# A routed two-expert layer on one core: turning the expert tiles through DRAM and VectorE instead of on TensorE

## The chip, the cores and the metric

One core of a Trainium2 chip. The metric is the device time of one execution in microseconds (us), the median of three runs. The engines are TensorE (PE, with its weight loads as PEld), VectorE (DVE), ScalarE (ACT), GpSimd (POOL) and SyncE (SP), which here only issues DMAs. A line number such as L1182 is a line of the kernel before.

## What is computed

The input is x, 8 x 512 tokens of 256 features. xn is its layer norm. The output is

```
x + attention(xn) + experts(xn)
attention: 16 heads of 16; A = tril(1 + q.k/4 + (q.k)^2/32), y = A v / rowsum(A), then y Wo^T
experts:   top 2 of 8 by xn Wg, weights by softmax over the two
           out[n] += w * ( silu(xn W1[e]) * (xn W2[e]) ) W3[e]      W1, W2: 256x512, W3: 512x256
```

Everything is float32.

## The kernel before

All engines run programs of their own, written out by hand (`sync_program`, `gpsimd_program`, `scalar_program`, `vector_program`, `tensor_program`), tied by semaphores: `p_*` are raised by PE, `v_*` by DVE, `a_*` by ACT, `g_*` by POOL, `d_*` by DMAs (16 for each that has landed). Within a program the order of the text is the order of the work; nothing overtakes.

The first 300 us do the attention in 32 quarters (`NQ`) and route the tokens. POOL scatters each token's normalised row (256 features, 8 gates, its number: `XW` = 272 words) twice into `xs_scr` in DRAM, once for each of its experts, so that the rows of one expert can be gathered. The second half works through `NT` = 71 tiles of 128 rows. A tile has one expert (`texp`, read into a register). The experts need at most 71 tiles; a tile beyond what they need is filled with spare rows and scattered to spare rows of `out`. The weights of the experts are loaded at the border of the two halves (`load_w12`, 16 units of 512 KB; `load_w3`, 8 of 512 KB), and each is split into a high and a low float32r part, since every product is made of three passes, high x high, high x low, low x high.

One tile t takes these steps:

- `gather(t)` (POOL, L485): an indirect DMA brings 128 rows into `xg`, a ring of `GR` = 4. `transpose_g(t)` (PE, L1171) turns them with two transposes into bank 4. `expert_x(t)` copies them as `xgh` (ACT, L619) and `xgl` (DVE, L979), and DVE copies the gates into `xw` (L984).
- `up(t, 0)` and `up(t, 1)` (PE, L1182): six matmuls each, for the silu branch and for the gate branch, into banks 0 to 3.
- `hs` is made by ACT's silu (L638) and DVE's product (L1009). `transpose_s(t)` (PE, L1191) turns it with four transposes into bank 5. `high_s` (ACT, L625) and `low_s` (DVE, L988) copy it as `sTh` and `sTl`. All of `xgh`, `xgl`, `hs`, `sTh`, `sTl` are single buffers.
- `down(t)` (PE, L1203): twelve matmuls into bank 6 or 7. `weigh_y(t)` (DVE, L996) multiplies by the row's gate into `yo` (two buffers). `scatter(t)` (POOL, L496) adds the rows to `out` in DRAM with an accumulating indirect DMA; it waits on `d_sc` for the scatter before, as two experts may hold the same token.

PE's order in the loop over t, the part that sets everything else, is:

```
up(t, 0); transpose_s(t - 1); up(t, 1); transpose_g(t + 1); down(t - 1)
```

DVE's is `low_s(t - 1)`, product of t, `expert_x(t + 1)`, for the first eight tiles also `w3_low(t + 1)` (L711) and `w12_low` (L706, up to t = 5), then `weigh_y(t - 1)`; ACT's follows it. POOL keeps four gathers ahead. SP has no work after its last load: at the border it issues `load_w3` (6 and 7 after `v_te`), `load_w12(14)`, waits for the last attention rows to reach `out` (`out_sent(LAST)`), issues `load_w12(15)` (L336), and then only waits for the scatters.

## Time and profile before

| | |
|---|---|
| median of 3 runs | 668.18 us (668.07 to 668.24) |
| the profiled execution, first to last instruction | 665.4 us |
| PE busy | 641.8 us, 96% |
| PE weight loads | 496.5 us, 75% |
| DVE busy | 410.6 us, 62% |
| ACT busy | 341.6 us, 51% |
| POOL busy | 344.1 us, 52% |
| DMA | 64.07 MB, mean 96 GB/s |

The profile gives the span of one execution, from its first to its last instruction; the time of a run is 2.8 us longer than that span. Busy shares are means over both halves of the kernel; the rows further down are of single stretches. A matmul's duration includes time in which the next one already streams, so the pace of PE is read from starts and from the chain of waits. The chain follows the work that ended last back from the end, each step to what released it.

### The profile page before, as it was taken

What the parts mean: (1) busy time and instruction counts of PE and PEld (TensorE: products, weight loads), DVE (VectorE), ACT (ScalarE), POOL (GpSimd) and SP (SyncE); (2) the same over time, 40 slices, a digit from 0 to 9 for tenths busy, and PEclk for the clock granted to TensorE, in tenths of its full rate; (3) what the DMA queues carried; (4) which work ended last, traced back from release to release, by engine and by line L of the source; (5) the groups of instructions that cost most, each with busy time, mean ns of one, the idle gap of its engine ahead of it and who ended that gap; (6) DMA issues with size and microseconds to landing.
All of it is one profiled execution on the core that took longest, in us unless ns stands there. A gap on an engine that the chain in (4) does not pass through costs nothing.

```text
span 665.4 us, 16423 instructions
## 1 busy us (share of the span) xinstructions
PE 641.8 (96%) x5414; PEld 496.5 (75%) x5414; DVE 410.6 (62%) x1067; ACT 341.6 (51%) x515; POOL 344.1 (52%) x381
## 2 busy tenths in 40 slices
PE   8899999999999999999999999999999999999994
PEld 7555666666666666657888888888888888888883
DVE  6777788787878585777975444444544445444452
ACT  3668878787877686766642232322323223232331
POOL 3265655546463736473465555455545555455542
PEclk9999999999999999999999999999999999999998
DMA  4653555554443435447633434333333433333332
GB/s 134 141 133 99 127 153 130 152 130 147 93 136 77 128 85 154 118 150 249 207 59 58 66 51 66 50 57 60 58 59 50 66 51 57 58 51 58 58 50 25
DMA packets 37775, 64.07 MB, mean 96 GB/s; under 512 B 8289, under 2 KB 25825, under 8 KB 37697
## 3 DMA queue, kind: packets, MB, share of 16 engines
q0 software_dynamic: 16704, 28.12, 22.0%
q1 hardware_dynamic: 20432, 34.24, 20.2%
q8 instruction: 50, 0.82, 0.5%
q10 hardware_dynamic: 560, 0.66, 0.3%
q14 instruction: 29, 0.23, 0.1%
HBM read 27.72 MB, written 22.68 MB: 76 GB/s over the span
## 4 chain that ended last, share of the span: by engine, by line
PE 87%; DVE 4%; DMA 2%; ACT 2%; issue 2%; SPq 1%; ACTq 0%; POOL 0%; POOLq 0%; DVEq 0%
PE banks L1182 29%; PE banks L1203 15%; PE banks L1056 10%; PE banks L1038 8%; PE banks L1076 7%; PE banks L1191 5%; PE banks L1085 4%; PE banks L1120 3%; PE banks L1171 2%; PE banks L1105 1%; PE banks L1111 1%; DMA K<-Kt 1%; ACT T L533 1%; DVE xTl L740 1%; PE banks L1094 1%
## 5 line engine op out<-in xcount | busy, mean ns | idle before, releaser
L496 POOL DMA_INDIRECT out<-yo,xw x71 | 112.2, 1581 | 154.4 <-DVE yo L996 76.6
L625 ACT ACTIVATE sTh<-banks 128x512 fp32r<-128x512 f32 x71 | 42.5, 598 | 192.4 <-PE banks L1191 186.6
L476 POOL TENSOR_SCALAR_AFFINE_SELECT T<-T 128x512 f32<-128x512 f32 x128 | 80.8, 642 | 108.5 <-ACT T L539 43.1
L988 DVE TENSOR_TENSOR sTl<-banks,sTh 128x512 fp32r<-128x512 f32 x71 | 49.0, 691 | 118.9 <-ACT sTh L625 118.9
L1182 PE MATMUL banks<-w12h,xgh 128*128 x284 | 118.0, 415 | 0.6 <-DVE xgl L979 0.6
L1182 PE MATMUL banks<-w12l,xgh 128*128 x284 | 112.2, 395 | 0.0
L1182 PE MATMUL banks<-w12h,xgl 128*128 x284 | 112.1, 395 | 0.0
L485 POOL DMA_INDIRECT xg<-xs_scr,glist x71 | 72.4, 1020 | 21.5 <-issue 20.0
L1056 PE MATMUL banks<-T,vau 128*17 128x512 f32 (+3 forms) x1024 | 75.6, 434 | 0.9 <-POOL T L476 0.9
L467 POOL DMA_INDIRECT xs_scr<-xb,slots x64 | 64.3, 1004 | 18.7 <-issue 10.0
L1038 PE MATMUL banks<-Q,K 32*128 32x256 f32 (+2 forms) x1024 | 70.5, 358 | 3.5 <-DMA K<-Kt 2.2
L525 ACT ACTIVATE T<-banks 128x1024 f32<-128x1024 f32 x64 | 62.1, 1026 | 12.5 <-PE banks L1038 11.9
L533 ACT ACTIVATE T<-banks 128x768 f32<-128x768 f32 x64 | 48.5, 810 | 27.2 <-PE banks L1038 27.2
L1182 PEld LDWEIGHTS banks<-w12h,xgl 128*128 128x128 f32 x284 | 53.3, 188 | 12.0
L1056 PEld LDWEIGHTS banks<-T,vau 128*17 128x17 f32 x1024 | 26.0, 97 | 46.3 <-issue 38.4
L1182 PEld LDWEIGHTS banks<-w12h,xgh 128*128 128x128 f32 x284 | 53.8, 189 | 7.8 <-issue 1.0
L1038 PEld LDWEIGHTS banks<-Q,K 32*128 32x128 f32 x1024 | 38.6, 183 | 27.1 <-ACT T L525 12.7
L1182 PEld LDWEIGHTS banks<-w12l,xgh 128*128 128x128 f32 x284 | 53.9, 190 | 6.3
L996 DVE TENSOR_SCALAR yo<-banks,xw 128x256 f32<-128x256 f32 x71 | 34.3, 483 | 39.0 <-PE banks L1203 31.2
L539 ACT ACTIVATE T<-banks 128x768 f32<-128x768 f32 x64 | 48.7, 810 | 18.0 <-PE banks L1038 16.1
L1009 DVE TENSOR_TENSOR hs<-banks,hs 128x512 f32<-128x512 f32 x71 | 49.1, 692 | 10.2 <-PE banks L1182 0.9
L1203 PE MATMUL banks<-w3h,sTh 128*128 x284 | 51.1, 302 | 0.8 <-ACT sTh L625 0.8
(174 smaller groups left out, 1222.3 us busy)
## 6 DMA issues: line engine op xcount, KB each, us to landing
Q<-Q SPq DMA_DIRECT2D x128, 64.0 KB, 2.4
w12r<-w SPq DMA_DIRECT2D x16, 512.0 KB, 4.2
out<-xa SPq DMA_DIRECT2D x16, 256.0 KB
w3r<-w SPq DMA_DIRECT2D x8, 512.0 KB, 8.7
K<-Kt SPq DMA_DIRECT2D x124, 32.0 KB
xa<-x SPq DMA_DIRECT2D x7, 512.0 KB, 4.7
xg<-xs_scr,glist POOLq DMA_INDIRECT x71
out<-yo,xw POOLq DMA_INDIRECT x71
```

What stands on the lines that cost most here:

```text
L467: e.indirect_dma_start(xs_d, bass.IndirectOffsetOnAxis(slots[:, k, 4 * b + blk:4 * b + blk + 1].bitcast(U32), 0), xb[b % 2][:, blk, :], No ...
L476: e.affine_select(out=v, in_=v, pattern=[[0, 4], [1, P]], compare_op=ALU.is_ge, fill=-1.0, base=0, channel_multiplier=-1).then_inc(s["g_mk ...
L485: e.indirect_dma_start(xg[:, t % GR, :], None, xs_d, bass.IndirectOffsetOnAxis(glist[:, t:t + 1].bitcast(U32), 0)).then_inc(s[f"d_g{t % GR ...
L496: e.indirect_dma_start(out, bass.IndirectOffsetOnAxis(xw[:, t % 4, NE:NE + 1].bitcast(U32), 0), yo[:, t % 2, :], None, compute_op=ALU.add) ...
L525: e.activation(T0[n % 2][:, 2 * h:2 * h + 2, :], banks[:, 2 * h:2 * h + 2, :], ACT.Square, scale=0.25, bias=1.0).then_inc(s["a_s"], 1)
L533: e.activation(T1[:, 2 * h:2 * h + 2, :], banks[:, 2 * h:2 * h + 2, 0:384], ACT.Square, scale=0.25, bias=1.0).then_inc(s["a_s"], 1)
L988: e.tensor_tensor(sTl[:], banks[:, 5, :], sTh[:].bitcast(F32), ALU.subtract).then_inc(s["v_st"], 1)
L1009: e.tensor_tensor(hs[:], banks[:, 2 * (t % 2) + 1, :], hs[:], ALU.mult).then_inc(s["v_mu"], 1)
L1038: i = e.matmul(banks[:, r, c0:c0 + w], K2[rr, g, h, jm * P:(jm + 1) * P], Q2[g][rr, h, p, 512 - w:512], start=(p == 0), stop=(p == 1))
L1056: i = e.matmul(banks[32 * r:32 * r + HA, 4, 512 - w:512], vau[b % 2][:, jm, 4 * qd + r, :], v[:, r, :], start=(jm == 0), stop=(jm == 2), s ...
L1182: i = e.matmul(banks[:, 2 * (t % 2) + m, :], a[:, k, :], w[:, bass.ds(expert[t] * 4 + (2 * k + m), 1), :], start=(k == 0 and n == 0), stop ...
L1203: i = e.matmul(banks[:, 6 + t % 2, 0:256], a[:, k * P:(k + 1) * P], w[:, bass.ds(expert[t] * 4 + k, 1), :], start=(k == 0 and n == 0), sto ...
```

## The change

Feature q of a row is now paired with its neighbour: the host lays the rows of `w12` and `w3` out as (P, 2) and (P, 4) where they were (2, P) and (4, P), so that partition p holds features 2p, 2p+1 (or 4p to 4p+3). A turn by 128 is then split in two. A store writes the tile's rows to DRAM (`x_turn`, `h_turn`) by column groups, a load reads them back so that 32 column positions and 4 row groups share the partitions, and DVE turns blocks of 32x32 from that buffer (`xq`, `hq`) into PSUM. ACT and DVE copy out of PSUM as before, with other access patterns.

- For tiles 4 (`TX`) and on, `store_x`, `load_x` (SP) and `turn_x` (DVE) take the place of `transpose_g`; for tiles 8 (`TS`) to 68 (below `TE`), `store_h`, `load_h` and `turn_s` that of `transpose_s`. Tiles 69 and 70 turn the product on PE again.
- From tile 8 on, `down` runs three tiles (`LAG`) behind `up`, `low_s` and `high_s` two tiles behind, and `expert_x` two tiles ahead.
- `xgh`, `xgl`, `hs`, `sTh`, `sTl` have two buffers and `xw` eight (`XR`); `xq` and `hq` have one.
- Gathers are issued in another order, up to nine tiles ahead of the scatter.
- `scatter(t)` waits for scatter t - 2, and for scatter t - 1 only where `held` says so: where t is the first tile of an expert, or a tile beyond those needed. `holds` computes that table on DVE in the first tile's iteration; POOL reads a word of it for each tile, and issues a small `mark` operation.
- `load_w3(6)` and `load_w3(7)` wait for `v_hold` in place of `v_te`. The descriptor scratch of POOL's DMAs is set to 4096 bytes.

The diff, cut to its core (`x_bank`, `s_bank` are the PSUM views; left out are the register and semaphore declarations and the constants of `holds`):

```diff
+TX = 4
+TS = 8
+TE = NT - 2
+LAG = 3
+XR = 8
...
+        sTh = rm.take("sTh", 1024, F32R, (2, 512))
+        sTl = rm.take("sTl", 1024, F32R, (2, 512))
...
+        hs = rx.take("hs", 1024, F32, (2, HID))
...
+        hq = rx.take("hq", 512)
+        xgh = rx.take("xgh", 512, F32R, (2, 256))
+        xgl = rx.take("xgl", 512, F32R, (2, 256))
+        xq = rx.take("xq", 256)
+        xw = rx.take("xw", XR * 16, F32, (XR, 16))
...
+        def x_bank(t):
+            v = banks[:, 4, 0:256]
+            return v if t < TX else v.rearrange("p (t j c) -> p j c t", t=4, j=2)
+
+        def x_turned(tile, t):
+            v = tile[:, t % 2, :]
+            return v if t < TX else v.rearrange("p (j c t) -> p j c t", j=2, t=4)
+
+        def s_bank(t):
+            v = banks[:, 5 if t < TE else 4 if t == TE else 2, :]
+            return v.rearrange("p (t k c) -> p k c t", t=4, k=4) if TS <= t < TE else v
+
+        def s_turned(tile, t):
+            v = tile[:, t % 2, :]
+            return v.rearrange("p (k c t) -> p k c t", k=4, t=4) if TS <= t < TE else v
...
-            e.wait_ge(s["v_te"], 1)
+            e.wait_ge(s["v_hold"], 1)
...
+            def store_x(t):
+                e.wait_ge(s[f"d_g{t % GR}"], 16 * (t // GR + 1))
+                e.dma_start(x_d[t % 4].rearrange("r p f -> p r f"),
+                            xg[:, t % GR, 0:D].rearrange("p (r f) -> p r f", r=4)).then_inc(s[f"d_sx{t % 2}"], 16)
+
+            def load_x(t):
+                e.wait_ge(s[f"d_sx{t % 2}"], 16 * ((t - TX) // 2 + 1))
+                if t > TX:
+                    e.wait_ge(s["v_tx"], t - TX)
+                e.dma_start(xq[:], x_d[t % 4].rearrange("r (c t) f -> (r c) (t f)", t=4)).then_inc(s["d_lx"], 16)
+
+            def store_h(t):
+                e.wait_ge(s["v_mu"], t + 1)
+                e.dma_start(h_d[t % 4].rearrange("r p f -> p r f"),
+                            hs[:, t % 2, :].rearrange("p (r f) -> p r f", r=4)).then_inc(s[f"d_sh{t % 2}"], 16)
+
+            def load_h(t):
+                e.wait_ge(s[f"d_sh{t % 2}"], 16 * ((t - TS) // 2 + 1))
+                if t > TS:
+                    e.wait_ge(s["v_th"], t - TS)
+                e.dma_start(hq[:], h_d[t % 4].rearrange("r (c t) f -> (r c) (t f)", t=4)).then_inc(s["d_lh"], 16)
+
+            store_x(TX)
+            for t in range(NT):
+                if TS <= t < TE:
+                    store_h(t)
+                if TS <= t - 1 < TE:
+                    load_h(t - 1)
+                if TX <= t + 3 < NT:
+                    load_x(t + 3)
+                if TX < t + 5 < NT:
+                    store_x(t + 5)
+            for u in range(2):
+                e.wait_ge(s[f"d_sc{u}"], 16 * ((NT + 1 - u) // 2))
 
...
-                    e.wait_ge(s["p_gt"], t - GR + 1)
+                    if t - GR < TX:
+                        e.wait_ge(s["p_gt"], t - GR + 1)
+                    else:
+                        e.wait_ge(s[f"d_sx{t % 2}"], 16 * ((t - GR - TX) // 2 + 1))
...
-                else:
-                    e.wait_ge(s["d_sc"], 16 * t)
-                e.indirect_dma_start(out, bass.IndirectOffsetOnAxis(xw[:, t % 4, NE:NE + 1].bitcast(U32), 0), yo[:, t % 2, :], None,
-                                     compute_op=ALU.add).then_inc(s["d_sc"], 16)
+                if t >= 3:
+                    if t == 3:
+                        e.wait_ge(s["v_hold"], 1)
+                    else:
+                        e.wait_ge(s["g_hold"], t - 3)
+                    count = 16 * ((t - 1) // 2)
+                    landed = e.value_load(held[0:1, t - 1:t], min_val=count, max_val=count + 16)
+                    e.wait_ge(s[f"d_sc{(t - 1) % 2}"], landed)
+                    e.tensor_tensor(mark[:], minus[:], minus[:], ALU.add).then_inc(s["g_hold"], 1)
+                    e.wait_ge(s[f"d_sc{t % 2}"], 16 * (t // 2))
+                elif t:
+                    e.wait_ge(s[f"d_sc{(t - 1) % 2}"], 16)
+                e.indirect_dma_start(out, bass.IndirectOffsetOnAxis(xw[:, t % XR, NE:NE + 1].bitcast(U32), 0), yo[:, t % 2, :], None,
+                                     compute_op=ALU.add).then_inc(s[f"d_sc{t % 2}"], 16)
...
-            for t in range(GR):
-                gather(t)
+            ahead = 0
             for t in range(NT):
-                if t + GR < NT:
-                    gather(t + GR)
+                upto = t + 5 if t == 0 else t + 6 if t < TS else t + 9
+                while ahead <= min(upto, NT - 1):
+                    gather(ahead)
+                    ahead += 1
                 scatter(t)
...
-            for t in range(NT + 1):
-                if t >= 1:
+            for t in range(NT):
+                if 1 <= t <= TS:
                     high_s(t - 1)
-                if t < NT:
-                    e.wait_ge(s["p_h"], t + 1)
-                    e.activation(hs[:], banks[:, 2 * (t % 2), :], ACT.Silu).then_inc(s["a_si"], 1)
+                e.wait_ge(s["p_h"], t + 1)
+                if 2 <= t < TS + 2:
+                    e.wait_ge(s["p_st"], t - 1)
+                elif TS + 2 <= t < TE + 2:
+                    e.wait_ge(s[f"d_sh{t % 2}"], 16 * ((t - 2 - TS) // 2 + 1))
+                e.activation(hs[:, t % 2, :], banks[:, 2 * (t % 2), :], ACT.Silu).then_inc(s["a_si"], 1)
                 if t == 0:
                     w3_high(0)
-                if t + 1 < NT:
+                if t + 1 < TX:
                     expert_x(t + 1)
+                if t - 2 >= TS:
+                    high_s(t - 2)
+                if TX <= t + 2 < NT:
+                    expert_x(t + 2)
                 if t + 1 < NE:
                     if t == 0:
                         e.wait_ge(s["p_av"], NQ)
@@ -651,10 +753,12 @@
                     elif u == 14:
                         e.wait_ge(s["p_o"], 2 * NBATCH)
                     w12_high(u)
+            high_s(NT - 2)
+            high_s(NT - 1)
...
+            def holds():
+
+                e.wait_ge(s["c_hold"], 2)
+                then(e.tensor_scalar(change[:], iota[:, 0:72], end[:, NE - 1:NE], None, ALU.is_ge))
+                then(e.tensor_tensor(part[:, 0:71], tf[:, 1:72], tf[:, 0:71], ALU.subtract))
+                then(e.tensor_tensor(change[:, 1:72], change[:, 1:72], part[:, 0:71], ALU.max))
+                then(e.scalar_tensor_tensor(held[:, 0:71], change[:, 1:72], 16.0, before[:, 0:71], ALU.mult, ALU.add), "v_hold")
...
+            def turn_x(t):
+                e.wait_ge(s["d_lx"], 16 * (t - TX + 1))
+                e.wait_ge(s["v_gt"], t)
+                e.transpose(banks[:, 4, 0:256], xq.rearrange("p (t m j) -> p t j m", t=4, j=2)).then_inc(s["v_tx"], 1)
+
+            def turn_s(t):
+                e.wait_ge(s["d_lh"], 16 * (t - TS + 1))
+                e.wait_ge(s["v_st"], t)
+                e.transpose(banks[:, 5, :], hq.rearrange("p (t m k) -> p t k m", t=4, k=4)).then_inc(s["v_th"], 1)
...
+            def gate_x(t):
                 e.wait_ge(s[f"d_g{t % GR}"], 16 * (t // GR + 1))
-                if t >= 4:
-                    e.wait_ge(s["d_sc"], 16 * (t - 3))
-                e.tensor_copy(xw[:, t % 4, :], xg[:, t % GR, D:XW]).then_inc(s["v_xw"], 1)
+                if t >= XR:
+                    e.wait_ge(s[f"d_sc{t % 2}"], 16 * ((t - XR) // 2 + 1))
+                e.tensor_copy(xw[:, t % XR, :], xg[:, t % GR, D:XW]).then_inc(s["v_xw"], 1)
...
             expert_x(0)
+            gate_x(0)
+            gated = 1
             step("y", LAST, 1)
             w12_low(UNITS)
             step("o", LAST, 0)
-            for t in range(NT + 1):
-                if t >= 1:
+            for t in range(NT):
+                if 1 <= t <= TS:
                     low_s(t - 1)
-                if t < NT:
-                    e.wait_ge(s["a_si"], t + 1)
-                    e.wait_ge(s["p_g"], t + 1)
-                    e.tensor_tensor(hs[:], banks[:, 2 * (t % 2) + 1, :], hs[:], ALU.mult).then_inc(s["v_mu"], 1)
-                if t + 1 < NT:
+                e.wait_ge(s["a_si"], t + 1)
+                e.wait_ge(s["p_g"], t + 1)
+                e.tensor_tensor(hs[:, t % 2, :], banks[:, 2 * (t % 2) + 1, :], hs[:, t % 2, :], ALU.mult).then_inc(s["v_mu"], 1)
+                if t + 1 < TX:
                     expert_x(t + 1)
+                if TS <= t - 2 < TE:
+                    turn_s(t - 2)
+                if TX <= t + 2 < NT:
+                    turn_x(t + 2)
+                while gated <= min(t + 1 if t < 2 else t + 3, NT - 1):
+                    gate_x(gated)
+                    gated += 1
+                if t - LAG >= TS:
+                    weigh_y(t - LAG)
+                if t - 2 >= TS:
+                    low_s(t - 2)
+                if TX <= t + 2 < NT:
+                    expert_x(t + 2)
                 if t == 0:
                     step("o", LAST, 1)
                     w3_low(0)
+                    holds()
                 if t + 1 < NE:
                     w3_low(t + 1)
                 if UNITS + 1 + t < 16:
                     w12_low(UNITS + 1 + t)
-                if t >= 1:
+                if 1 <= t <= TS:
                     weigh_y(t - 1)
+            low_s(NT - 2)
+            weigh_y(NT - 3)
+            low_s(NT - 1)
+            weigh_y(NT - 2)
+            weigh_y(NT - 1)
...
-            for t in range(1, NT + 1):
-                if t < NT:
-                    expert_of(t)
-                    up(t, 0)
+            for t in range(1, NT):
+                expert_of(t)
+                up(t, 0)
                 if t == 1:
                     for m in range(3):
                         e.wait_ge(s[f"m{m}"], USED[m])
-                transpose_s(t - 1)
-                if t < NT:
-                    up(t, 1)
-                if t + 1 < NT:
+                if t <= TS or t == TE + 1:
+                    transpose_s(t - 1)
+                up(t, 1)
+                if t + 1 < TX:
                     transpose_g(t + 1)
-                if t <= NE:
-                    e.wait_ge(s["v_tl"], t)
-                down(t - 1)
+                if t <= TS:
+                    if t <= NE:
+                        e.wait_ge(s["v_tl"], t)
+                    down(t - 1)
+                elif t - LAG >= TS:
+                    down(t - LAG)
+            transpose_s(NT - 1)
+            for t in range(NT - LAG, NT):
+                down(t)
...
-        "w12": w12.reshape(NE, 2, P, 2, HID).transpose(2, 0, 1, 3, 4).reshape(P, NE * 4, HID),
-        "w3": np.asarray(L0_ffn_W3).reshape(NE, 4, P, D).transpose(2, 0, 1, 3).reshape(P, NE * 4, D),
+        "w12": w12.reshape(NE, P, 2, 2, HID).transpose(1, 0, 2, 3, 4).reshape(P, NE * 4, HID),
...
-    nc = bacc.Bacc("TRN2", target_bir_lowering=False, num_devices=1)
+    nc = bacc.Bacc("TRN2", target_bir_lowering=False, num_devices=1, dynamic_dma_scratch_size=4096)
```

## Rows read from the trace of the kernel before

**Rows 1.** Stretches: length, busy PE, PEld, DVE, ACT, POOL, clock, DMA share, GB/s

```profile
341.00:652.00 311.00, 311.00 (x1911) 271.02 (x1910) 146.41 (x320) 94.29 (x192) 164.21 (x127) 1.00 0.35 56
```

**Rows 2.** Chain of waits, one tile: start us, us, what

```profile
644.27 1.39 PE banks L1182 x6
645.66 0.44 PE banks L1191 x4
646.10 1.40 PE banks L1182 x6
647.49 0.22 PE banks L1171 x2
647.71 1.43 PE banks L1203 x12
```

**Rows 3.** Timeline of DVE and of PE, first expert tiles: start us, us, engine

```profile
296.76 0.22 DVE L772 CAST glist<-banks 128x72 int32<-128x72 f32 x1
...
321.09 0.41 DVE L979 TENSOR_TENSOR xgl<-banks,xgh 128x256 fp32r<-128x256 f32 x1
...
323.13 1.22 DVE L706 TENSOR_TENSOR w12l<-w12r,w12h 128x1024 fp32r<-128x1024 f32 x1
324.27 0.48 DVE L996 TENSOR_SCALAR yo<-banks,xw 128x256 f32<-128x256 f32 x1
...
326.25 0.64 PE L1203 MATMUL banks<-w3h,sTl 128*128 x4
```

**Rows 4.** Timeline of PE and of POOL, the end

```profile
652.20 0.63 PE L1203 MATMUL banks<-w3h,sTh 128*128 x4
...
654.69 1.55 POOL L496 DMA_INDIRECT out<-yo,xw  x1 [3.09 <-DVE yo L996]
659.25 1.55 POOL L496 DMA_INDIRECT out<-yo,xw  x1 [3.00 <-DMA out<-yo,xw]
```

**Rows 5.** Groups by line on DVE, 340 to 650 us: busy, mean ns, idle before

```profile
L1009 DVE TENSOR_TENSOR hs<-banks,hs 128x512 f32<-128x512 f32 x64 | 44.3, 692 | 9.1 <-PE banks L1182 0.2
...
L996 DVE TENSOR_SCALAR yo<-banks,xw 128x256 f32<-128x256 f32 x64 | 30.9, 484 | 36.9 <-PE banks L1203 29.9 <-DMA out<-yo,xw 7.0
L979 DVE TENSOR_TENSOR xgl<-banks,xgh 128x256 fp32r<-128x256 f32 x64 | 26.5, 414 | 0.0
L984 DVE COPY xw<-xg 128x16 f32<-128x16 f32 x64 | 11.2, 175 | 0.0
```

**Rows 6.** Groups by line on POOL, 341 to 650 us

```profile
L496 POOL DMA_INDIRECT out<-yo,xw x64 | 101.2, 1581 | 125.4 <-DVE yo L996 70.2 <-DMA out<-yo,xw 42.4 <-PE banks L1171 7.1
L485 POOL DMA_INDIRECT xg<-xs_scr,glist x62 | 61.5, 992 | 18.9 <-issue 17.4 <-DVE xw L984 1.5
```

**Rows 7.** DMA queues, 289 to 294 us and 304 to 320 us: packets, MB, share

```profile
q1 hardware_dynamic: 272, 0.26, 16.4%
...
q1 hardware_dynamic: 1759, 4.99, 86.3%
```

**Rows 8.** DMA queues, 359 to 648 us

```profile
q0 software_dynamic: 11399, 15.98, 35.0%
```

**Rows 9.** DMA issues: KB each, us from issue to landing

```profile
wo_r<-wo SPq DMA_DIRECT2D x1, 256.0 KB, 2.6
...
out<-zero SPq DMA_DIRECT2D x1, 128.0 KB, 5.1
```

**Rows 10.** Instructions of line 336 on SP: ns, first and last start

```profile
L336 SPq DMA_DIRECT2D w12r<-w x16: 328/484/1644, 39.0 to 320.2; - x16
```

**Rows 11.** DMA, 318 to 328 us in 40 slices of 0.25 us

```profile
GB/s 447 414 426 406 418 434 401 446 393 442 410 410 442 410 361 311 328 442 360 393 279 156 148 119 205 139 33 156 204 217 17 0 0 0 0 0 0 0 0 0
```

**Rows 12.** Stretches at the end, columns as in rows 1

```profile
658.00:660.00 2.00, 0.00 (x0) 0.00 (x0) 0.00 (x0) 0.00 (x0) 0.76 (x1) 1.00 0.01 1
...
662.00:665.40 3.40, 0.00 (x0) 0.00 (x0) 0.00 (x0) 0.00 (x0) 0.00 (x0) 0.50 0.18 28
```

**Rows 13.** DMA queues, 656 to 665 us

```profile
q0 software_dynamic: 288, 0.26, 26.9%
```

More of the change, by code:

```diff
@@ L157, in build @@
         banks = ctx.enter_context(nc.psum_tensor("banks", [P, 8, 512], F32))
-        rm = Region(344, A0)
+        rm = Region(344, Q1)
         xg = rm.take("xg", GR * XW, F32, (GR, XW))
-        xgh = rm.take("xgh", 256, F32R, (2, P))
-        xgl = rm.take("xgl", 256, F32R, (2, P))
-        hs = rm.take("hs", 512)
-        sTh = rm.take("sTh", 512, F32R)
-        sTl = rm.take("sTl", 512, F32R)
-        yo = rm.take("yo", 512, F32, (2, D))
-        xw = rm.take("xw", 64, F32, (4, 16))
-        rq = Region(344, A0)
+        sTh = rm.take("sTh", 1024, F32R, (2, 512))
+        sTl = rm.take("sTl", 1024, F32R, (2, 512))
+        yo = rm.take("yo", 512, F32, (2, D))
+        rx = Region(Q1, A0)
+        hs = rx.take("hs", 1024, F32, (2, HID))
+        at_hq = rx.at
+        hq = rx.take("hq", 512)
[3 more added lines that the diff above has]
+        xw = rx.take("xw", XR * 16, F32, (XR, 16))
+        held = rx.take("held", 72, I32)
+        mark = rx.take("mark", 4)
+        rh = Region(at_hq, at_hq + 512)
+        before_i = rh.take("before_i", 72, I32)
+        before = rh.take("before", 72)
+        change = rh.take("change", 72)
+        rq = Region(344, Q1)
         K2 = rq.take("K2", 2048, F32R, (2, 2, 512))
@@ L446, in gpsimd_program @@
             e.memset(zero[:], 0.0).then_inc(s["c_z"], 1)
+            e.wait_ge(s["c_hold"], 1)
+            e.tensor_copy(before[:], before_i[:]).then_inc(s["c_hold"], 1)
             e.wait_ge(s["c_z"], 1)
@@ L1181, in up @@
                     for n, (a, w) in enumerate(((xgh, W12h), (xgh, W12l), (xgl, W12h))):
[L1182 removed]
+                        i = e.matmul(banks[:, 2 * (t % 2) + m, :], a[:, t % 2, k * P:(k + 1) * P], w[:, bass.ds(expert[t] * 4 + (2 * k + m), 1), :],
                                      start=(k == 0 and n == 0), stop=(k == 1 and n == 2))
@@ L1202, in down @@
                     for k in range(4):
-                        i = e.matmul(banks[:, 6 + t % 2, 0:256], a[:, k * P:(k + 1) * P], w[:, bass.ds(expert[t] * 4 + k, 1), :],
+                        i = e.matmul(banks[:, 6 + t % 2, 0:256], a[:, t % 2, k * P:(k + 1) * P], w[:, bass.ds(expert[t] * 4 + k, 1), :],
                                      start=(k == 0 and n == 0), stop=(k == 3 and n == 2))
```

53 lines of the change are left out of this document (33 added, 20 removed).

## The prediction

> **What bounds the kernel now.** The sums are against the profiled execution (span 665.4 us); the median of the runs is 668.2 us, 2.8 us more, and I carry that 2.8 unchanged. From the page I took the busy shares, then a table of stretches, then the chain of waits. From 341 to 652 us TensorE (PE) is busy for the whole of the stretch at full granted clock, VectorE (DVE) for 47%, GpSimd (POOL) for 53% [rows 1]. So in the expert part PE sets the pace and everything else fits beside it. The chain shows one tile, five pieces: six up matmuls 1.40, four turns of the gated product 0.44, six up matmuls 1.39, two turns of the gathered rows 0.22, twelve down matmuls 1.43, together 4.88 us [rows 2]. Two ends differ. At the beginning DVE runs almost without a gap, because it splits weights too [rows 3]; at the end the last scatter waits for the one before it to land [rows 4].
>
> **What it removes.** Turns of rows leave PE for tiles 4 to 70, 67 x 0.22 = 14.7 us; turns of the gated product for tiles 8 to 68, 61 x 0.44 = 26.8 us [rows 2]. Together **-41.5 us**, and PE's tile becomes 1.40 + 1.39 + 1.43 = 4.22 us. It is all gain only if each new helper keeps a period of 4.22 us.
>
> **DVE per tile.** Today two 128x512 operations (hs and sTl) of 0.692 and 0.414 + 0.484 + 0.175, in all 2.46 us [rows 5]. It adds a 32x32 turn of 128x512 and one of 128x256. The trace has none; the nearest rows are the DVE operations of the same size that touch PSUM, 0.69 and 0.41 us. Lower end half of these (no second operand to read), upper end twice, should a turn run at half rate. Taken: those rows, 1.1, sum 3.6 us (3.0 to 4.7). ACT gets no new instruction, only another source to wait for.
>
> **POOL per tile.** Gather 0.99 and scatter 1.58 with 0.3 ahead of each [rows 6] are 3.2 us; the new register read and the 128x4 `mark` operation are as small as DVE's 0.175 us copy [rows 5]; from nothing to 0.3 each: 3.2 to 3.8 us, taken 3.5. It fits under 4.22. A scatter that landed alone took 4.56 us until the next one started [rows 4]; that serial chain would no longer fit, and the second scatter in flight removes it except where an expert changes (seven times, one tile's delay, covered by the spare POOL time) and at the end (below).
>
> **The DMA trips.** Per tile 128 KB go out in 512 packets of 256 bytes and come back in 128 of 1 KB; 256 KB go out in 512 packets of 512 bytes and come back in 128 of 2 KB. A stretch with stores in 1 KB packets gives 16.4% x 5 us x 16 / 272 = 48 ns a packet; one with mostly 4 KB packets gives 86.3% x 16 us x 16 / 1759 = 125 ns for 2.84 KB in the mean [rows 7]. A line through both gives 15, 26, 48 and 92 ns for the four sizes, so 7.7 + 13.3 + 6.1 + 11.8 = 38.9 us over 16 engines, 2.4 us per tile. That is also about the low end (bytes at the 1 KB rate: 2.3). The high end is that no packet costs less than a 1 KB one: 4.2 us. I take 2.4, since the two rows differ almost in proportion to bytes. Gathers and scatters already take 35.0% x 289 us / 59.3 tiles = 1.7 us [rows 8]. Sum 4.1 of 4.22 us: it just fits, and it is the thinnest margin here. The Trainium skill speaks against the change: its page "DMA: Bandwidth & Descriptors" (Specifications) asks for at least 512 bytes per transfer for line rate and says that below this the engine reads, modifies and writes. No packet of data under 1 KB is in this trace, so it can't be checked; the sum by that rule is worked as the first rival, without it.
>
> **The loop through one buffer.** `hq` is single, so load_h(t-1) waits until turn_s(t-2) is done, and turn_s(t-1) waits for the load. A lone 256 KB load took 2.6 us from issue to landing, and 128 KB among other transfers 5.1 [rows 9]. Ahead of it in SP's queue is store_h(t), issued 0.6 us earlier with 0.8 us of data; with that and a share of the scatter I take 3.3. Then 0.7 + 0.1 + 3.3 = 4.1 us, again just under 4.22. SP itself issues four DMAs of some 0.5 us [rows 10], 2 us. As both margins are thin, I put **+5 us** (0.08 x 61) for periods that slip; nothing to 40 are the ends (40: the period stays 4.88).
>
> **The beginning.** `holds` puts four small dependent operations (0.22 us each, as the 0.22 us cast) [rows 3] on DVE at about 313 us, ahead of low_s(0), for which PE already waits: **+0.9**. SP reaches store_x(4) only behind load_w12(15), which it issues at 320.2 because it first waits for the last output rows [rows 10]. The engines are full until about 323.3 us [rows 11], so store_x(4) lands near 325, load_x(4) (2.6 and some) near 327.7, and turn_x(4) ends near 328.1. DVE wants it in its iteration 2, right after xgl at 321.5 plus 0.9 [rows 3]. Queued behind it on DVE are the gate copies, xgl(4), two weight splits (which wait for ACT, itself stuck at expert_x(4)), weigh_y(1) and low_s(2): 0.4 + 0.5 + 1.7 + 1.2 + 0.4 + 0.6, low_s(2) ends at 332.9. PE wants it at the third part of down(2), near 326.9. **+6.0 us** PE idle; bounds 2 (the landings 2 us quicker, the splits overlapped) and 9. After it DVE's iterations of 5.1 us against PE's 4.66 cost **+1.3** until the splits end. PE at rest loses its clock: at the end of the trace PE does nothing from 658 us on, the granted clock is still 1.00 up to 660, and from 662 it is 0.50, the 1.2 GHz level [rows 12]. I put **+1.0** (0 to 3). The skill's page "TensorE: Matmul & The Clock Gate" (What's actually happening) states the same drop to half at rest; the trace agrees.
>
> **The end.** The down projections are three tiles behind, but at tiles 9 and 10 PE does no down, so its total work is the same and the last up matmuls end 2 x 1.43 = 2.9 us earlier than the savings alone give. From the end of the last up matmul, p = 652.2, the execution before needs 13.15 us. Now weigh_y(67) follows down(67) at p + 2.0 and scatter(67) starts at p + 2.4. By counting the reference's inputs, the experts fill 9, 9, 8, 8, 8, 8, 8 and 9 tiles, 67 in all; tiles 67 to 70 are padding, and `held` makes each of their scatters wait for the one before. Three steps of 4.56 + 0.15 and the 6.1 us that the last scatter needs to the end [rows 4] give p + 22.6. That is +9.4 - 2.9 = **+6.5 us**.
>
> **Sum**: -41.5 + 0.9 + 6.0 + 1.3 + 1.0 + 6.5 + 5 = -20.8, from 668.2 to **647 us**.
>
> **Rivals.** *DMA engines are the bound (slower than before).* If packets of 256 bytes cost as much as 1 KB ones, store_x takes 1.54 instead of 0.48, the tile 2.4 + 1.05 + 1.7 = 5.2 us, and the total is 668.2 - 41.5 + 15.7 + 61 x 0.98 = 702; if part of the 1.7 is waiting (two scatters by themselves were 26.9% x 9 us = 2.4, 1.2 each [rows 13]), about 4.9 and 684. It turns slower where the period passes 4.64 (25.8 us of net gain over 61 tiles is 0.42), that is at 2.9 us of new DMA time per tile. For it: the sum without it is already 98% of the period. Against: 400 GB/s with the engines full [rows 11], while the new sum is about 1.06 MB in 4.22 us, 250 GB/s. *The hq loop.* The load takes 3.6 to 4.2 under its own traffic: periods 4.4 to 5.0, total 653 to 690. For: 5.1 us in a contended stretch. Against: 2.6 alone. *The ends cost little*: the stall of DVE doesn't reach PE and the periods hold: 668.2 - 41.5 + 6.5 + 0.9 + 2 = 636. *DVE turns at half rate*: 4.7 us a tile, 61 x 0.48 in place of the 5, 671. That the turns stay on PE can't be: the code issues none there.
>
> **How the numbers follow.** Forecast (640 to 654) 0.42, ends cheap 0.10, hq loop 0.20 (0.13 faster, 0.02 same, 0.05 slower), DMA bound 0.20 (0.01 same), DVE slow 0.08 (0.02 faster, 0.02 same, 0.04 slower). Changes within 0.2%, 1.3 us, are about what a measurement of this kernel can't tell from none. Faster 0.42 + 0.10 + 0.13 + 0.02 = 0.67, same 0.05, slower 0.28. The range is 635 to 686: it leaves out only the worse part of the DMA case and a little below. The cases on the faster side alone lie between 635 and 660.
>
> **What would show it.** In the changed profile: the chain of a middle tile has 1.40, 1.39, 1.43 and no turn; DVE turns of about 0.69 and 0.41; PE idle of some 6 us once between 322 and 333; four scatters 4.7 us apart at the end; DMA share near 0.9 in the middle with some 230 GB/s or more; landing of load_h near 3.3. PE idle in each tile released by sTh or sTl, whose own releaser is the DMA of `hq`, shows the loop; DMA share at 0.98 or over with periods near 5 shows the first rival; DVE busy near 100% the last. The forecast is wrong if the middle period isn't 4.2 to 4.4.

## The result, and the profile after

The changed kernel takes 689.64 us in the median of four runs (687.1 to 691.13), the kernel before 668.21 beside it (668.07 to 669.03): 1.0314 times as long, 95% interval 1.0292 to 1.0337. The forecast of 647 us and its range to 686 were both wrong, and so was the direction. The profiled execution has a span of 686.9 us (688.6 as timed), against 665.4 before. Single runs of the kernels below that lie over 1.5% above a kernel's fastest are left out of the ratios; one does, 683.8 us for the turn without a step. The page of the changed kernel, its counts, chain and the group of the turn:

```profile
span 686.9 us, 16518 instructions
PE 630.1 (92%) x5036; PEld 468.2 (68%) x5036; DVE 485.1 (71%) x1199; ACT 335.4 (49%) x515; POOL 356.4 (52%) x451
DMA packets 123794, 113.63 MB, mean 165 GB/s; under 512 B 46688, under 2 KB 104032, under 8 KB 123712
...
PE 39%; DMA 30%; DVE 12%; issue 11%; ACT 3%; SPq 2%; DVEq 1%; POOL 1%; ACTq 0%; POOLq 0%
DMA hq<-h_turn 23%; PE banks L1199 10%; PE banks L1181 8%; PE banks L1219 7%; DVE banks L1097 6%; PE banks L1228 3%; PE banks L1263 3%; DMA out<-yo,xw 2%; PE banks L1326 2%; PE banks L1248 1%; DMA out<-xa 1%; PE banks L1254 1%; ACT T L620 1%; DVE hs L1133 1%; PE banks L1348 1%
...
L1097 DVE STREAM_TRANSPOSE banks<-hq 128x512 f32<-128x512 f32 x61 | 67.2, 1101 | 82.1 <-DMA hq<-h_turn 82.0
```

PE is 11.7 us less busy, yet the span is longer. Up matmuls (L1326) and down matmuls (L1348) have nearly left the chain, and a DMA, the load of `hq`, holds 23% of it.

The start of the product `hs(t)` on DVE is a good milestone for tile t, since both kernels do it once a tile. Read from the DVE timelines of the two kernels:

| stage | before | after | difference |
|---|---|---|---|
| up to hs(0) | 309.5 | 312.1 | +2.6 |
| hs(0) to hs(8) | 40.2 | 50.6 | +10.4 |
| hs(8) to hs(64) | 273.4 | 274.7 | +1.3 |
| hs(64) to hs(70) | 29.4 | 27.8 | -1.6 |
| hs(70) to the end | 12.9 | 21.7 | +8.8 |

Most of the first 2.6 us doesn't belong to the change: in this execution the granted clock was 0.66 between 20 and 30 us. Of the ten kernels below, which have the same first part or nearly, the four at full clock there reach hs(0) at 308.5 to 309.2 us, the four at 0.83 at 309.6 to 310.6, and the two at 0.66 at 310.6 and 311.1. Everything else is two fixed costs at the ends and a middle that gained nothing.

**The middle.** Stretches of the changed kernel (columns as in [rows 1]):

```profile
316.00:341.00 25.00, 18.48 (x91) 15.55 (x90) 17.45 (x31) 10.52 (x18) 6.20 (x5) 0.86 0.72 221
...
400.00:500.00 100.00, 93.77 (x493) 75.73 (x492) 71.35 (x146) 28.74 (x63) 55.66 (x61) 1.00 0.94 216
```

PE is busy 94% instead of 100% (a matmul's duration reaches into the next one, so its waits look shorter than they are); the DMA share went from 0.35 to 0.94. Between 400 and 660 us the chain of waits has almost no matmul in it. A piece of it (start us, us, what):

```profile
442.34 3.62 DMA hq<-h_turn
445.96 0.46 issue
446.42 1.11 DVE banks L1097
...
447.59 4.23 DMA hq<-h_turn
451.82 0.02 issue
451.84 1.12 DVE banks L1097
...
453.03 3.68 DMA hq<-h_turn
```

Load, turn, load, turn: the one buffer `hq` is a loop. Read from the timelines of SP and DVE over 430 to 600 us, SP issues the load of `hq` within 0.2 us of the end of the turn before it in 35 of 36 tiles, and DVE stands waiting for it in 35. From its issue to the start of its turn a load takes 3.71 us in the mean (2.6 to 4.5), the turn 1.10, and some 0.1 lies between: 4.9 us a tile. (The chain doesn't follow this loop all the way; in places it goes over the store of the product, with some 2.4 us of "issue" in front of the same load.) Between hs(24) and hs(64) the period is 4.93 us, where it was 4.88. The DVE groups of 400 to 600 us say how that looks on DVE (busy us, mean ns, idle before):

```profile
L1097 DVE STREAM_TRANSPOSE banks<-hq 128x512 f32<-128x512 f32 x41 | 45.2, 1102 | 54.9 <-DMA hq<-h_turn 54.9
...
L1092 DVE STREAM_TRANSPOSE banks<-xq 128x256 f32<-128x256 f32 x41 | 17.2, 420 | 0.3 <-DMA xq<-x_turn 0.3
```

DVE stands 1.3 to 1.4 us a tile in front of `turn_s`, waiting for the load, and the turn itself takes 1.10 us, not 0.69. The turn of half as many elements takes 0.42. The DMA queues of the same stretch (packets, MB, share of the 16 engines):

```profile
q1 hardware_dynamic: 54600, 32.02, 57.6%
q0 software_dynamic: 7755, 10.97, 35.7%
```

**The beginning.** DVE of the changed kernel (start us, us, what):

```profile
315.48 0.25 DVE L984 TENSOR_SCALAR change<-iota,end 128x72 f32<-128x72 f32 x1
...
316.31 0.23 DVE L987 SCALAR_TENSOR_TENSOR held<-change,before 128x71 int32<-128x71 f32 x1
...
324.90 0.41 DVE L1101 TENSOR_TENSOR xgl<-banks,xgh 128x256 fp32r<-128x256 f32 x1
330.52 0.46 DVE L1092 STREAM_TRANSPOSE banks<-xq 128x256 f32<-128x256 f32 x1 [5.21 <-DMA xq<-x_turn]
```

The four operations of `holds` are there; then DVE is idle for 5.21 us in front of `turn_x(4)`, with weight splits queued behind it. PE feels it at 329.4 us (start us, us, what):

```profile
328.07 0.40 PE L1326 MATMUL banks<-w12l,xgh 128*128 x1
328.31 0.40 PE L1326 MATMUL banks<-w12h,xgl 128*128 x1
...
334.08 1.22 PE L1348 MATMUL banks<-w3h,sTh 128*128 x4 [4.68 <-DVE w3l L815]
...
337.25 0.63 PE L1326 MATMUL banks<-w12l,xgh 128*128 x1
337.68 0.63 PE L1326 MATMUL banks<-w12h,xgl 128*128 x1
```

It waits 4.68 us for the low part of a weight that DVE splits behind `turn_x(4)`, and comes back slow: up matmuls start 0.43 us apart instead of 0.24. The granted clock is 0.50, the 1.2 GHz level, from 334 to 340 us, and 0.96 from 340 to 343.

**The end.** POOL of the changed kernel:

```profile
664.89 1.55 POOL L582 DMA_INDIRECT out<-yo,xw  x1 [0.46 <-POOL mark L578]
...
669.71 1.55 POOL L582 DMA_INDIRECT out<-yo,xw  x1 [0.70 <-POOL mark L578]
...
682.27 1.55 POOL L582 DMA_INDIRECT out<-yo,xw  x1 [0.15 <-issue]
```

These are scatters 66, 67 and 70; 68 and 69 start at 673.99 and 678.08. From scatter 67 on, each `mark` is released by the landing of the scatter before, so they come some 4.35 us apart. Five scatters stand behind the last up matmul, which ends at 664.9 us, where [rows 4] had two behind theirs.

### The profile page after: what moved, and what is told of

Same layout as the page of the kernel before. It is cut to its first block, busy times and chain, and to the rows that moved or that the text cites. A ratio compares the mean times of both kernels' runs of the same rounds, so it can differ in the third digit from the quotient of the medians.

```text
span 686.9 us, 16518 instructions
## 1 busy us (share of the span) xinstructions
PE 630.1 (92%) x5036; PEld 468.2 (68%) x5036; DVE 485.1 (71%) x1199; ACT 335.4 (49%) x515; POOL 356.4 (52%) x451
## 3 DMA queue, kind: packets, MB, share of 16 engines
q0 software_dynamic: 16704, 28.12, 21.6%
## 4 chain that ended last, share of the span: by engine, by line
PE 39%; DMA 30%; DVE 12%; issue 11%; ACT 3%; SPq 2%; DVEq 1%; POOL 1%; ACTq 0%; POOLq 0%
DMA hq<-h_turn 23%; PE banks L1199 10%; PE banks L1181 8%; PE banks L1219 7%; DVE banks L1097 6%; PE banks L1228 3%; PE banks L1263 3%; DMA out<-yo,xw 2%; PE banks L1326 2%; PE banks L1248 1%; DMA out<-xa 1%; PE banks L1254 1%; ACT T L620 1%; DVE hs L1133 1%; PE banks L1348 1%
## 5 line engine op out<-in xcount | busy, mean ns | idle before, releaser
L1326 PE MATMUL banks<-w12h,xgh 128*128 x284 | 118.8, 418 | 8.1 <-issue 4.3
L1097 DVE STREAM_TRANSPOSE banks<-hq 128x512 f32<-128x512 f32 x61 | 67.2, 1101 | 82.1 <-DMA hq<-h_turn 82.0
L1326 PE MATMUL banks<-w12h,xgl 128*128 x284 | 111.6, 393 | 0.0
L1326 PE MATMUL banks<-w12l,xgh 128*128 x284 | 111.5, 393 | 0.0
L1326 PEld LDWEIGHTS banks<-w12h,xgh 128*128 128x128 f32 x284 | 53.7, 189 | 28.1 <-issue 19.1
L1348 PE MATMUL banks<-w3h,sTh 128*128 x284 | 51.1, 302 | 20.1 <-ACT sTh L720 14.0
L578 POOL TENSOR_TENSOR mark<-minus 128x4 f32<-128x4 f32 x68 | 13.3, 196 | 105.6 <-DMA out<-yo,xw 87.2
L1348 PEld LDWEIGHTS banks<-w3h,sTh 128*128 128x128 f32 x284 | 41.9, 189 | 37.9 <-issue 35.6
L1326 PEld LDWEIGHTS banks<-w12h,xgl 128*128 128x128 f32 x284 | 53.6, 189 | 11.7
L1326 PEld LDWEIGHTS banks<-w12l,xgh 128*128 128x128 f32 x284 | 53.7, 189 | 8.7
L626 ACT ACTIVATE T<-banks 128x768 f32<-128x768 f32 x64 | 48.8, 810 | 18.5 <-PE banks L1181 16.5
```

Source lines behind the costliest of these rows:

```text
L626: e.activation(T2[:, 2 * h:2 * h + 2, :], banks[:, 2 * h:2 * h + 2, P:512], ACT.Square, scale=0.25, bias=1.0).then_inc(s["a_s"], 1)
L1097: e.transpose(banks[:, 5, :], hq.rearrange("p (t m k) -> p t k m", t=4, k=4)).then_inc(s["v_th"], 1)
L1326: i = e.matmul(banks[:, 2 * (t % 2) + m, :], a[:, t % 2, k * P:(k + 1) * P], w[:, bass.ds(expert[t] * 4 + (2 * k + m), 1), :], start=(k == ...
L1348: i = e.matmul(banks[:, 6 + t % 2, 0:256], a[:, t % 2, k * P:(k + 1) * P], w[:, bass.ds(expert[t] * 4 + k, 1), :], start=(k == 0 and n == ...
```

## Experiments

Theory L: the middle is the loop through `hq`, load plus turn. Rival D: the 16 DMA engines are full. Two more questions are what the small packets cost and whether the costs at the ends can be had back. Periods are read between hs(24) and hs(64) of each profile (or the two milestones named), as above. Expectations speak of the kernels by what they change; those of the first four were written before any of them had run.

**A second buffer for `hq`.** The load waits for the turn two tiles back.

```diff
-        hq = rx.take("hq", 512)
+        hq = rx.take("hq", 1024, F32, (2, 512))
...
-                if t > TS:
-                    e.wait_ge(s["v_th"], t - TS)
+                if t > TS + 1:
+                    e.wait_ge(s["v_th"], t - TS - 1)
```

Each buffer has its own load semaphore, and for room the descriptor scratch is 2048 bytes; that wasn't changed by itself.

> The changed kernel with hq in two buffers, so that load_h(t) waits for turn_s(t-2) instead of turn_s(t-1) (the descriptor scratch of POOL's DMAs is halved to 2048 bytes to make room). Loop theory: the period of 4.88 us is load_h (3.7) + turn_s (1.10) + 0.1 in series, and falls to what PE allows, 4.2 to 4.4; total about 689.6 - 59 x 0.55 = 657. Engine theory: the 16 DMA engines, busy 0.94 of the time, are the bound; the period can't fall below 0.94 x 4.88 = 4.6, and the total stays at 674 or more, with a DMA share of 0.98 or over.

Measured: 664.6 us (659.07 to 667.73, seven runs), 0.9938 of before (0.9903 to 0.9974), 25 us better than the change. Stretch and queues from 430 and 400 us on:

```profile
430.00:600.00 170.00, 163.78 (x906) 140.37 (x905) 133.35 (x264) 53.68 (x112) 105.19 (x115) 1.00 0.98 235
```

```profile
q1 hardware_dynamic: 59496, 34.83, 65.7%
q0 software_dynamic: 8542, 12.00, 31.9%
```

The period falls to 4.52 us with the same traffic per tile, so full engines were not what held the change at 4.93: theory L holds for it. The idle time before `turn_s` goes from 1.4 to 0.2 us a tile. But the 4.22 us of PE aren't reached, and the total lies between the two forecasts, 657 and 674. The engines are now busy for 0.98 of the time, 0.98 x 4.52 = 4.4 us of engine time a tile, so D is one candidate for what comes next. It is a soft bound: the same packets took 0.94 x 4.93 = 4.6 us in the change, so share times period isn't a fixed amount of work.

**A turn without a step in its reads.** `turn_s` reads 32 neighbouring words where it took every fourth. It turns other 32x32 blocks than the reference needs, so the gated product that goes into the down projection is a permuted one; the work is otherwise the same.

```diff
-                e.transpose(banks[:, 5, :], hq.rearrange("p (t m k) -> p t k m", t=4, k=4))
+                e.transpose(banks[:, 5, :], hq.rearrange("p (t k m) -> p t k m", t=4, k=4))
```

> The changed kernel, but turn_s reads hq without a step (k outside m instead of m outside k); the blocks it turns are then not those of the reference, all transfers and counts are the same. It is to tell whether the 1.10 us of turn_s, against 0.42 for half as many elements in turn_x, comes from the step of 4 words of its reads: then it falls to about 0.70. Loop theory: the period falls by those 0.4 us, total about 689.6 - 59 x 0.4 = 666. Engine theory: turn_s gets shorter but the waits for hq grow by the same, total 676 or more.

Measured: 679.48 us (671.88 to 683.8), ratio 1.0202 (1.0163 to 1.0241). The group of the turn, 430 to 600 us, beside the 1102 ns above:

```profile
L1097 DVE STREAM_TRANSPOSE banks<-hq 128x512 f32<-128x512 f32 x38 | 27.4, 722 | 17.0 <-DMA hq<-h_turn 16.8
```

The step in the reads costs 0.38 us per turn, and the period from hs(24) on is 4.57, which is 0.36 less than the change's, as a loop would have it. As a test of L this run is weak, though. From hs(8) to hs(24) the period is 4.85, as in the change (4.84); from 430 to 600 us DVE waits for `hq` in only half of the tiles, with the engines at 0.99. The profiled execution (671.88) was the fastest of the four, and the median is 10 us under the change where L said 24: it lies where the engine theory had put it, at 676 or more. The price of the step is shown; that its removal is worth as much in every execution is not.

**Rows turned on PE, product through DRAM.** It takes one of the two trips away, and with it the stall at tile 4.

```diff
-TX = 4
+TX = NT
...
-            store_x(TX)
...
-                upto = t + 5 if t == 0 else t + 6 if t < TS else t + 9
+                upto = t + 5 if t == 0 else t + 6 if t < TS else t + 8
```

> Half of the change alone: the gathered rows are turned on PE in all tiles (no store_x, load_x, turn_x), the gated product still goes through DRAM with the single hq. PE's tile is 4.44 us. The stall at tile 4 and its slow clock go, 8 us. Loop theory with the load slowed by the other transfers: without 0.85 us of DMA time per tile the load takes 2.9 to 3.2, the loop 4.1 to 4.4, PE is the bound, total 689.6 - 8 - 59 x 0.44 = 656. If the load's time is its own and not contention (3.7 stays), the period stays 4.88 and the total is about 681. DMA share falls to about 0.75.

Measured: 656.31 us (655.71 to 659.98), ratio 0.9852 (0.9819 to 0.9885). Its chain, and its stretch:

```profile
508.79 3.48 DMA hq<-h_turn
512.27 0.02 issue
512.29 1.11 DVE banks L1096
```

```profile
430.00:600.00 170.00, 169.17 (x971) 148.25 (x970) 120.93 (x224) 54.07 (x112) 104.21 (x113) 1.00 0.80 176
```

The engines are at 0.80, far from full, and still the chain from 430 to 600 us is load and turn. The load takes 3.35 us in the mean (2.5 to 4.3) instead of 3.71, and the period, 4.54, is shorter by the same 0.4. So the loop alone, without full engines, holds a period above PE's 4.44; and the load was shorter with less traffic around it. The total of 656 was forecast, but with PE as the bound and a load of 2.9 to 3.2; that part was wrong.

**The same, with a second buffer for `hq`.** `xgh` and `xgl` go back to one buffer each to make room.

```diff
-TX = 4
+TX = NT
...
-        hq = rx.take("hq", 512)
-        xgh = rx.take("xgh", 512, F32R, (2, 256))
-        xgl = rx.take("xgl", 512, F32R, (2, 256))
+        hq = rx.take("hq", 1024, F32, (2, 512))
+        xgh = rx.take("xgh", 256, F32R, (1, 256))
+        xgl = rx.take("xgl", 256, F32R, (1, 256))
```

> As the kernel with the gathered rows on PE, and hq in two buffers (xgh and xgl are single again, as before, to make room). Both theories say that nothing but PE bounds the middle: period 4.44, total 668.2 - 61 x 0.44 + 1.2 (holds) + 6.5 (end) = 649. It is equal to the kernel with a single hq if the loop there already fits under PE's period, and faster than it by what the loop still costs.

Measured: 651.55 us (650.54 to 652.9), ratio 0.9769 (0.9748 to 0.9789). Its chain:

```profile
508.73 2.75 PE banks L1326 x12
511.49 0.23 PE banks L1315 x2
511.71 1.44 PE banks L1348 x12
```

Here the chain is PE alone, 2.75 + 0.23 + 1.44 = 4.42, and the period 4.44: exactly the 0.44 us of the product's turns less than before. The descriptor scratch is 4096 bytes here, so the second buffer helps without that change too. From hs(69) to the end it needs 26.0 us, against 17.8 before.

**Eight tiles' rows turned on PE first.** One number of the change, `TX`, goes from 4 to 8, so that the first load of `xq` comes after the weights.

```diff
-TX = 4
+TX = 8
```

> The changed kernel with TX = 8: the rows of tiles 4 to 7 are turned on PE too, so nothing waits for the DMA queue behind the last weights. If the start costs what the prediction says, the time from DVE's product of tile 0 to that of tile 8 falls from 50.6 us to about 42 (40.2 before, and 1.1 for holds, 0.7 for the first turns on DVE), the clock stays full, and the total falls by 8.5 us to about 681; the middle keeps its period of 4.93. If the stall only hides a wait that comes anyway (weights that are late), it falls by less than 3.

Measured: 675.96 us (674.09 to 678.03), ratio 1.0123 (1.0091 to 1.0155). The stretch that held the stall:

```profile
316.00:341.00 25.00, 24.59 (x146) 21.64 (x147) 22.89 (x38) 14.72 (x23) 14.18 (x11) 1.00 0.63 166
```

PE is busy for 24.59 of 25 us instead of 18.48, and the clock is full. From hs(0) to hs(8) it takes 42.0 us instead of 50.6: 8.6 us back. The middle stays as it was (period 4.92, DMA share 0.94). Between the two profiled executions 13.2 us lie; 3.6 more of them are before the first tile, where the change's profile had its slow stretch, and 0.9 behind hs(70).

**The stores in long packets.** Beside the second `hq` buffer, rows are stored in packets of 1 KB and products in packets of 2 KB. The layout in DRAM is then another, so rows and products that are turned are not those of the reference; bytes, loads and turns are the same in number.

```diff
-                e.dma_start(x_d[t % 4].rearrange("r p f -> p r f"),
-                            xg[:, t % GR, 0:D].rearrange("p (r f) -> p r f", r=4))
+                e.dma_start(x_d[t % 4].rearrange("r (a b) f -> (r a) (b f)", b=4),
+                            xg[:, t % GR, 0:D])
```

> The changed kernel with two buffers for hq (and a descriptor scratch of 2048 bytes), and with both stores written to DRAM row by row, in packets of 1 KB and 2 KB in place of 256 and 512 bytes: the same bytes, a quarter of the packets. The blocks that DVE turns are then not those of the reference. It tells packets from bytes in the DMA engines' bound (share 0.98, period 4.52 with two buffers). If small packets cost extra (21 and 27 ns against 12 and 23 for their bytes), the engines' time per tile falls from 4.4 to about 4.0 and the period to PE's 4.2 to 4.25, total 664.6 - 59 x 0.3 = 647. If it is bytes, period and total stay at 4.5 and 664.

Measured: 663.22 us (658.95 to 664.95), ratio 0.9929 (0.9897 to 0.9961), the same as with short packets within the spread. Queues of 430 to 600 us, and its chain:

```profile
q1 hardware_dynamic: 21985, 30.10, 58.7%
q0 software_dynamic: 7298, 10.28, 32.2%
```

```profile
501.76 4.76 DMA xq<-x_turn
...
515.16 3.92 DMA xq<-x_turn
```

The short packets do cost something: q1 takes 58.7% x 4.48 = 2.63 us a tile instead of 65.7% x 4.52 = 2.97. But the period falls by 0.04 only, with the engines at 0.92 and 4.1 us of engine time in it, which is less than PE's 4.22. The theory that short packets keep it from 4.22 missed by 16 us. The chain names another candidate: the rows have one buffer too, `xq`. Its load is issued within 0.2 us of the end of `turn_x` in nearly every tile (39 of 40 between 430 and 600 us), behind 256 KB for `hq` in SP's order; DVE has to wait for it in 20 of 41 tiles, and there it takes 4.1 us in the mean (3.6 to 5.6).

**The rows' load and turn first.** In both kernels with two `hq` buffers, the load of `xq` goes ahead of that of `hq` on SP, and `turn_x` ahead of `turn_s` on DVE. With the long packets:

```diff
+                if TX <= t + 3 < NT:
+                    load_x(t + 3)
                 if TS <= t - 1 < TE:
                     load_h(t - 1)
-                if TX <= t + 3 < NT:
-                    load_x(t + 3)
```

> As the kernel with two hq buffers and stores in long packets (other layout in DRAM, so the turned blocks are not the reference's), but the load of xq goes ahead of the load of hq on SP and turn_x ahead of turn_s on DVE. If the loop through the single xq holds the period at 4.48 us (its load is queued behind 256 KB for hq), the load shortens, the period falls to PE's 4.22 to 4.3 and the time to 663 - 61 x 0.2 = about 651 us. If it is full engines or DVE's order as a whole that holds it, it stays at 4.45 or more and 663 us.

Measured: 662.43 us (661.51 to 664.12), ratio 0.9926 (0.9903 to 0.995), period 4.48 as before the move. Its chain:

```profile
501.83 4.11 DMA xq<-x_turn
...
506.50 4.68 DMA xq<-x_turn
511.21 0.47 DVE banks L1092
...
512.16 3.69 DMA hq<-h_turn
```

And with the short packets:

> The same two moves (xq's load and turn first) in the kernel with two hq buffers and short packets, which had a period of 4.52 us at a DMA share of 0.98, 4.43 us of engine time per tile. If the engines are a bound of their own, the period can't go below about 4.43: 659 to 665 us. If only the xq loop held it, it goes to 4.22 to 4.3 like the kernel with long packets, about 651 us.

Measured: 672.05 us (669.1 to 674.38, seven runs), ratio 1.005 (1.0019 to 1.0081), 7 us slower than without the move, and above both forecasts; period 4.60, DMA share 0.98. The load of `xq` hardly got shorter by going first, and what was won in front of `turn_x` was lost in front of `turn_s`: in 170 us DVE idles 3.2 instead of 10.0 us in front of the one and 14.7 instead of 5.3 in front of the other with long packets, 5.3 instead of 8.0 and 15.9 instead of 6.2 with short ones. So the order of the loads isn't it. DVE now waits for `hq` oftener (in 26 of 41 tiles with long packets), but the loop through `xq` is still there. Whether two buffers for `xq` as well would reach 4.22 stays open: it wasn't tried. The rival that several loads in flight are simply slow at this share stands beside it. With both trips and short packets no run had a period under 4.43, the forecast of D, but none of them was without the loop through `xq` either.

**Rows through DRAM, product turned on PE.** The other half of the change, with `TX` = 8.

```diff
-TS = 8
-TE = NT - 2
+TS = NT
+TE = NT + 9
```

> The other half of the change alone, from tile 8: only the gathered rows go through DRAM and DVE, the gated product is turned on PE in all tiles and the down projection is one tile behind. PE's tile is 1.40 + 0.44 + 1.39 + 1.43 = 4.66 us. Its loop (load 2.7, turn 0.42) and the DMA engines (1.07 + 1.5 us per tile) are far below. Total 668.2 - 63 x 0.22 + 1.1 (holds) + 1 (end) = 656.5. If the trips of the rows disturb the gathers and scatters, so that POOL or yo sets the pace, it stays above 662.

Measured: 660.51 us (657.32 to 661.36), ratio 0.9877 (0.9844 to 0.991). Chain of one tile:

```profile
506.18 1.39 PE banks L1320 x6
507.57 0.47 PE banks L1330 x4
508.05 1.40 PE banks L1320 x6
509.44 1.42 PE banks L1342 x12
```

PE sets the pace at 4.71 us with the DMA share at 0.60. The rows' turns leave PE for 0.17 us a tile, less than the 0.22 of [rows 2]. It came out 4 us above expectation; a short clock dip at the start is part of that (0.93 from 316 to 341 us).

**A better version.** The product's trip alone, with two `hq` buffers, and both ends mended: padding tiles alternate between two blocks of 128 spare rows, so that a scatter has to wait for the one before only where a new expert begins, and `holds`, now two operations, is done a step earlier on DVE.

```diff
-                then(e.tensor_tensor(change[:, 1:72], change[:, 1:72], part[:, 0:71], ALU.max))
-                then(e.scalar_tensor_tensor(held[:, 0:71], change[:, 1:72], 16.0,
+                then(e.scalar_tensor_tensor(held[:, 0:71], part[:, 0:71], 16.0,
...
-    args.append(nc.dram_tensor("out", (NTOK + P, D), F32, kind="ExternalOutput").ap())
+    args.append(nc.dram_tensor("out", (NTOK + 2 * P, D), F32, kind="ExternalOutput").ap())
```

> The kernel with rows on PE and two buffers for hq, and two repairs. Tiles beyond those needed use one of two blocks of spare rows by the parity of the tile, so that their scatters need not wait for each other (held is 16 more only at a new expert). holds is two operations and stands ahead of the output of the attention's last block, where DVE waits anyway. If the serial chain of scatters is what the end costs, the time from DVE's product of tile 69 to the end falls from 26.0 to about 18.5 us, and the start by 1; total 651.5 - 8.5 = 643. If the end is set by the down projections three tiles behind, it falls by 3 or less, to 648.

Measured: 644.96 us (644.61 to 646.89), ratio 0.9666 (0.9644 to 0.9689), the fastest of all, 23 us under before and 45 under the change. POOL at its end:

```profile
629.46 1.55 POOL L589 DMA_INDIRECT out<-yo,xw  x1 [0.46 <-POOL mark L585]
...
632.45 1.55 POOL L589 DMA_INDIRECT out<-yo,xw  x1 [0.70 <-POOL mark L585]
...
635.28 1.55 POOL L589 DMA_INDIRECT out<-yo,xw  x1 [0.46 <-POOL mark L585]
```

From hs(0) to hs(1) it takes 6.2 us, as before the change. The last scatters now follow 2.8 to 3.0 us apart instead of 4.35, and hs(69) to the end takes 21.6 us instead of 26.0. I had expected 18.5. Of the 3.8 us that stay over the 17.8 of before, 2.8 are PE's: its last down projection ends 12.0 us after hs(69) instead of 9.2, because it lags three tiles behind.

## Why the prediction was wrong, step by step

- **What leaves PE** (-41.5): right, as far as PE goes. No turn is in its middle, and where nothing else limits, the period fell by what was removed (4.88 to 4.44 with the product's turns gone).
- **The loop through one buffer**: this step failed, and it decides. I put 0.7 + 0.1 + 3.3 = 4.1 us and +5 us for slips. Measured were 1.10 for the turn and 3.71 for the load, 4.9 together, so all of the saving came back as waiting. Two terms were too small, each by 0.4. The turn was priced by rows of the same size without a step in their reads; the bound of 4.7 us for all of DVE's work took a slow turn in, but I never carried it from DVE's sum into the loop, where each 0.1 us of it counts at once. The load leaned on the row of 2.6 us, whose engines had been idle and were shared only with a 512 KB load issued 0.4 us behind it; at a share of 0.94 the row under traffic (5.1 for half the bytes) should have weighed more. The rival "the hq loop" (periods 4.4 to 5.0, 653 to 690 us) is what happened; with it at 0.20 I had the mechanism but put the likeliest case just on the good side of two thin margins. That the DMA rival's 4.9 us and 684 come near the measured numbers too is chance: the second `hq` buffer changes nothing for the engines and takes 0.4 us off the period.
- **The DMA sum** (4.1 of 4.22 us): 4.6 measured in the change, 4.4 at the second `hq` buffer. The product's trip took 39.3% x 4.54 = 1.8 us of q1 where only it was left (1.6 by the steps), the rows' trip 22.5% x 4.71 = 1.06 where only they went through DRAM (0.9), the gathers and scatters 1.4 to 1.8 (1.7). Each term was near; the sum was nevertheless over PE's 4.22. Whether it alone would have held the period above 4.22 isn't shown. In the price for a packet the rival "DMA engines are the bound" was wrong: the rows' 1.06 x 16 = 17 us, less 128 packets at 48 ns, leave (17 - 6.1) / 512 = 21 ns for a packet of 256 bytes, an estimate nearer to the 15 of the line than to the 48 of a 1 KB packet. The Trainium skill's page "DMA: Bandwidth & Descriptors" (Specifications) asks for transfers of at least 512 bytes for line rate. The trace agrees in the direction: by these estimates a packet of 256 bytes moved 12 bytes per ns and one of 1 KB 21, where the rival took 5. Storing in long packets (in place of those of 256 and of 512 bytes) brought 0.34 us a tile of engine time and almost no time.
- **DVE and POOL per tile**: not limits. DVE works 71% and POOL 56% of 400 to 500 us. DVE's sum was 3.6 and is 71.35 / 20.3 tiles = 3.5.
- **The beginning** (0.9 + 6.0 + 1.3 + 1.0 = 9.2, less 0.9 of turns saved): 10.4 measured. The mechanism was right: `store_x(4)` is issued at 323.31 us behind `load_w12(15)`, takes 5.12 us to land, its load 2.06, and `turn_x(4)` blocks DVE's queue and through it a weight split. PE idled 4.68 us (6.0), in front of down(2) and for that split, not for `low_s(2)` at its third part, as I had it. The store was later than I put it, the load faster, and the clock dearer: a down projection, six up matmuls and four turns at half pace cost nearer 3 us than 1. `TX` = 8 takes 8.6 us of it away.
- **The end** (p + 22.6): p + 22.0 measured, with p = 664.9. The sum is right and its parts are not: scatter 67 started at p + 4.8 instead of p + 2.4, because it had to wait for scatter 66, while the steps were 4.2 instead of 4.7 and the last one needed 4.6 us to the end instead of 6.1.

By stages, 42.3 us separate the expected span from the measured one: 33.7 in hs(8) to hs(64), where 32.4 us of gain were forecast (56 tiles x 0.66, less their part of the 5) and 1.3 of loss came; 2.6 before the first tile; 2.1 in the beginning; 3.9 in the tail.

## What to carry to other kernels

An operation that is moved off the bound engine can become a loop of its own: its period is the load plus the use of its staging buffer, and that must be added up with the latency under the traffic that the change itself makes, before the busy shares are looked at. With one buffer the load and the turn never overlap; a second buffer was worth 25 us here, and with half of the trips dropped besides, 38. Fixed costs at both ends (a queue blocked by the first use, a series of padding scatters) are small per item, and here they took 19 us (10.4 and 8.8), where the change was to save 41.5.
